# Turning a self attention head's masked weights one slot later while cross attention runs (transformer stack, one core)

## The reference, cut to what matters

```
# 1. cross attention, 16 heads of 16, x against 4096 context rows
energy = einsum('nqhd,nkhd->nhqk', q, k)
attn   = softmax(energy / E**0.5)
x = x + (einsum('nhqk,nkhd->nqhd', attn, v)) @ Wo.T + bo
# 2. self attention, 16 heads, only the 64 largest scores of a row count
scores = einsum('bhqd,bhkd->bhqk', q, k) / 4
top_scores, top_idx = top_k(scores, 64)
x = x + (softmax(top_scores) @ v[top_idx]) @ Wo.T + bo
```

## Time and profile before

| | |
|---|---|
| median of 3 runs | 1667.11 us (1654.56, 1667.11, 1667.49) |
| span of the profiled execution | 1653.0 us |
| busy PE / DVE / ACT | 1379.1 / 1325.5 / 976.1 us (83%, 80%, 59%) |
| mean granted clock of PE | 0.900 of full speed |
| head 0 of self attention starts | 215.1 us |
| first head after cross attention (p = 45) starts | 841.6 us |
| head 63 ends | 1127.9 us |

### The profile page before, as it was taken

How to read it: one execution, slowest core, us unless ns; L and a number is a source line. 1 busy time by engine, 2 the same in 40 slices (tenths; PEclk the granted TensorE clock), 3 DMA queues, 4 the chain that set the end, 5 groups by cost and what they waited for, 6 DMA issues and landing times. The chain is left out here.

```text
span 1653.0 us, 31583 instructions
## 1 busy us (share of the span) xinstructions
PE 1379.1 (83%) x11762; PEld 853.6 (52%) x11762; DVE 1325.5 (80%) x3968; ACT 976.1 (59%) x1579; POOL 273.9 (17%) x253
## 2 busy tenths in 40 slices
PE   8999899998999998999968797698669789464646
PEld 4555556665665665666644583475246336222213
DVE  1221178999799998989998999999988988888993
ACT  6678676776677776778743533456485366334420
POOL 4100012222132222222222121211100100100000
PEclk9999998999999999999979898799779899676567
DMA  7645341444022211220104122125436326223220
GB/s 150 157 116 129 66 92 38 99 96 92 14 40 53 52 21 34 53 36 18 40 24 160 52 87 67 39 80 171 131 100 172 114 60 172 72 57 109 85 56 7
DMA packets 96855, 132.67 MB, mean 80 GB/s; under 512 B 20192, under 2 KB 80872, under 8 KB 93744
## 3 DMA queue, kind: packets, MB, share of 16 engines
q1 hardware_dynamic: 96688, 130.50, 31.7%
HBM read 124.95 MB, written 5.51 MB: 79 GB/s over the span
## 5 line engine op out<-in xcount | busy, mean ns | idle before, releaser
L1325 ACT ACTIVATE attn_arena<-ps 128x1024 f32<-128x1024 f32 x512 | 496.5, 1022 | 205.9 <-PE ps L411 204.7
L1906 DVE MATCH_REPLACE8 attn_late<-attn_top,attn_late 128x256 f32<-128x256 f32 x1024 | 410.9, 409 | 0.0
L1903 DVE MAX8 attn_top<-attn_late 128x8 f32<-128x256 f32 x1024 | 380.8, 413 | 24.3 <-ACT attn_late L1347 24.3
L411 PE MATMUL ps<-attn_arena 32*128 32x256 f32 x4096 | 375.1, 408 | 8.7 <-ACT attn_arena L1325 4.3
L411 PEld LDWEIGHTS ps<-attn_arena 32*128 32x128 f32 x4096 | 253.7, 188 | 77.3 <-issue 42.7
L425 PE MATMUL ps<-attn_arena 128*32 128x256 f32 x4096 | 280.8, 391 | 1.3 <-issue 0.7
L1213 POOL TENSOR_SCALAR attn_late<-attn_late 128x512 f32<-128x512 f32 x64 | 95.6, 1494 | 602.4 <-DVE attn_late L1906 602.4
L425 PEld LDWEIGHTS ps<-attn_arena 128*32 128x32 f32 x4096 | 108.5, 110 | 135.2 <-issue 76.5
L1472 ACT ACTIVATE attn_arena<-attn_late,attn_arena 128x255 f32<-128x255 f32 x256 | 108.0, 496 | 89.4 <-DVE attn_late L1746 56.8
L686 PE MATMUL ps<-attn_arena 128*128 128x256 f32 x512 | 130.0, 400 | 17.5 <-ACT attn_arena L1427 17.4
L664 PE MATMUL ps<-attn_arena,attn_q 128*128 128x512 f32 x256 | 135.8, 660 | 5.7 <-ACT attn_arena L1413 5.5
(11 more groups left out here) (235 smaller groups left out, 1643.7 us busy)
## 6 DMA issues: line engine op xcount, KB each, us to landing
attn_arena<-ctxT SPq DMA_DIRECT2D x124, 256.0 KB, 4.7
attn_arena<-maskT SPq DMA_DIRECT2D x32, 512.0 KB, 4.4
attn_arena<-ctx SPq DMA_DIRECT2D x32, 512.0 KB, 4.1
attn_late<-rows SPq DMA_DIRECT2D x256, 64.0 KB, 2.3
attn_arena<-ctxV SPq DMA_DIRECT2D x15, 1024.0 KB, 13.0
attn_late<-wide SPq DMA_DIRECT2D x64, 128.0 KB, 2.9
attn_early<-wide SPq DMA_DIRECT2D x64, 128.0 KB, 3.5
wide<-attn_early SPq DMA_DIRECT2D x16, 256.0 KB, 3.0
```

Source lines behind the costliest of these rows:

```text
L411: mm = pe.matmul(ps[:, first + j - 2 * i, u * S:(u + 1) * S], kx[n % 2][rows, k0:k0 + P], qpad[rows, n % GROUPS, b * S:(b + 1) * S], start ...
L1325: act.activation(probs[m % 2][:, 2 * i:2 * i + 2], ps[:, first:first + 2, :], ACT.Exp, scale=1.0 / 16.0).then_inc(exp_done, 1)
L1903: dve.max(top[:, t, turn], s[:, i, t] if turn == 0 else work[:, i, t]).then_inc(picked, 1)
L1906: dve.match_replace(work[:, i, t], top[:, t, turn], s[:, i, t] if turn == 0 else work[:, i, t], LOW).then_inc(picked, 1)
```

## The change

While cross attention still runs (`crossing(p)`, true for p up to 44) the four steps of head `done` move. PE: `turn_pm` from slot 0 to the end of slot 1, behind `scores(p + 1)`; `products` from slot 2 to slot 3, behind that slot's `turn_acc`, `make_qk`, `make_v` or `project` and ahead of what `DUE` places there. ACT: `take_pT` from slot 1 to slot 2, behind `take_scores(p + 1)`; `take_sums` from the end of slot 3 to the start of slot 0 of the next period. DVE: `divide_self` from turn 1 to turn 3. The instructions, their number and their tiles are the same. From p = 45 on everything stands where it stood.

```diff
+def crossing(p):
+    return cross_it(p, 0) is not None
@@ PE
                     if slot == 0:
-                        if 0 <= done < B * H:
+                        if 0 <= done < B * H and not crossing(p):
                             turn_pm(done)
...
                             turn_x(h)
+                        if 0 <= done < B * H and crossing(p):
+                            turn_pm(done)
                     if slot == 2:
-                        if 0 <= done < B * H:
+                        if 0 <= done < B * H and not crossing(p):
                             products(done)
...
                                 make_qk(b, (q + 2) // 4)
+                        if 0 <= done < B * H and crossing(p):
+                            products(done)
@@ ACT
                     m = cross_it(p, slot)
+                    if slot == 0 and p >= 2 and crossing(p - 1):
+                        take_sums(p - 2)
...
                     if slot == 1:
-                        if 0 <= done < B * H:
+                        if 0 <= done < B * H and not crossing(p):
                             take_pT(done)
...
                             take_scores(p + 1)
+                        if 0 <= done < B * H and crossing(p):
+                            take_pT(done)
                         if ending and d == 2:
-                            take_sums(done) if done >= 0 else None
                             take_qk(h, 0)
                     if slot == 3:
                         if ending and d == 0:
-                            take_sums(done) if done >= 0 else None
                             take_misc(general[:, h:h + 1], M_[:, 0:1], "bad", h)
                         elif ending and d == 2:
                             take_scores(p + 1)
-                        elif 0 <= done < B * H:
+                        if 0 <= done < B * H and not crossing(p):
                             take_sums(done)
@@ DVE
-                    if 0 <= p - 2 < B * H and (p - 2) % HG == HG - 1:
+                    if 0 <= p - 2 < B * H and (p - 2) % HG == HG - 1 and not crossing(p - 1):
                         divide_self(p - 2)
...
                 if turn == 3:
+                    if p >= 2 and (p - 2) % HG == HG - 1 and crossing(p - 1):
+                        divide_self(p - 2)
```

## The result

The changed kernel took 1680.94 us (median of 4 runs, 1679.91 to 1682.30), the kernel before 1660.84 us (4 runs, 1648.70 to 1667.49): a ratio of 1.0157, 95% interval 1.0113 to 1.0200. It is slower, as forecast. The ratios and their intervals here rest on fast runs alone (those within 1.5% of the same kernel's fastest), while a median takes all runs, so a ratio isn't the quotient of the two medians beside it.

What follows compares the result with a forecast made beforehand. DVE's search was taken to bound heads 0 to 13, PE with its exponentials heads 17 to 44, DVE from 45. Terms +3 - 3 + 26 + 0 gave +26, span 1679, some 1681 us; 1688 was forecast, range 1664 to 1708.

Steps and rivals of the forecast that it cites:

- Slots of the plain head: PE's four slots in a plain crossing head: 2.41, 4.62, 2.41, 3.98 us, 13.42 against 12.29, +1.13 us a head.
- The value 1.64 for L571 and L579 together: Slot 1's scores plus transposes on PE: 1.64 us taken, 0.59 if they overlapped the next L411 as before.
- Heads 17 to 44: Stretch where PE is the nearer bound: 28 x 13.42 plus other blocks gives 412.8 us against 387.2, +25.6.
- Heads 0 to 13: Stretch paced by DVE, which hides the start of PE's growth: between 0 and +6.7 us, +3 taken.
- Heads 14 to 16: Stretch helped by fewer waits for masked weights and `project`: between -6 and +3 us, -3 taken.
- Waits moved: ACT's and DVE's moved steps in the crossing are covered; if one cover failed, 0 to +0.3 us a head.
- After head 44: Rest of the kernel, where DVE sets the pace: nothing moves, 0 us.
- From the span to the median: Whole kernel: span 1679 means some 1681 us for this execution; 1688 taken, between that and 1693.
- DVE's waits for copied scores: In the crossing, DVE would wait for copied scores in nearly every head, together over 50 us.
- A: Rival, crossing: PE's waits and half speed go, nothing else is paid; 17 us faster, 1650; chance 0.07.
- B: Rival, crossing: spells and waits go (29 us), offsetting re-packed slots (32 us); some +8, 1675; chance 0.25.
- C: Rival, crossing: half speed stays, nothing of 15.3 us comes back; +41, 1708; chance 0.12.

Runs made afterwards that it cites:

- e3: Changed kernel with `turn_pm` ahead of `scores(p + 1)` in slot 1 instead of behind it; 1653.05 us, ratio 1.0003 to the kernel before.
- e1: Kernel before with only `turn_pm` moved, to behind slot 1's scores; 1643.72 us, ratio 0.9919 to the kernel before.
- e2: Changed kernel with `turn_pm` back in slot 0 and `take_pT` back in slot 1; 1651.28 us, ratio 0.9997 to the kernel before.
- e8: Changed kernel, unchanged, run again; 1679.19 us, ratio 1.0182 to the kernel before.
- e4: Kernel before with only `turn_pm` moved, to slot 1 ahead of `scores(p + 1)`; 1645.92 us, ratio 0.9945 to the kernel before.

## Why the prediction was right, and where it wasn't

The forecast (slower, 1688 us, 1664 to 1708) came out at 1680.94. Its mechanism is shown: the two pieces came to stand in slots that wait themselves, the transposes parted the scores from their neighbour, and the two empty slots gave their time to nobody. That the sum of the parts came so near is luck in part: +26 was forecast for the span and +27.8 measured, but the terms are off by +4.3 (heads 0 to 13), +1.8 (14 to 16), -5.5 (17 to 44), +3.9 (after) and -2.3 us (ahead of head 0), and cancel.

- *Slots of the plain head.* Forecast 2.41, 4.62, 2.41, 3.98; measured 2.32, 4.62, 2.32, 3.97. The value 1.64 for L571 and L579 together was taken right from its two bounds (0.59 and 1.64). e3 shows what the other would have meant.
- *Heads 17 to 44.* Forecast 412.8 us, measured 407.3 and 407.0. The mis-sized term is the empty slot: 2.41 us came from a slot behind which L411 waited 0.25 us for the exponential; behind the empty slots of the changed kernel it waits 0.16, and they take 2.32. Twice 0.09 or 0.10 us in 28 heads is 5.3 us, the whole difference. The other terms held as a sum only, 407.3 - 28 x 13.23 = 36.9 us against the 37 counted: a block of eight matmuls costs 1.72 to 1.82 us (14.95 - 13.23 with `make_qk`), not 1.93, and the small ones more than 10.
- *Heads 0 to 13.* Forecast +3, measured +7.3 and +3.4. One account fits both; it is an estimate. e1 and e2, without a spell there, took 181.6 us, close to DVE's own busy time there (181.3), so the spell of 10.2 us and the gap of 1.42 us ahead of it cost the kernel before some 5.8 of its 187.4. The changed kernel without spell and without its own gap (1.4 us, last section) is at 189.4. The moved pieces so cost some 7.8 us, above my upper bound of 6.7, and the lost spell took 5.8 off that in both comparisons (7.8 - 5.8 + 1.4 = 3.4 in e8). The +3 came near the +3.4 of e8 for that reason, not for mine.
- *Heads 14 to 16.* Forecast -3, measured -1.2 and -3.4; the first execution holds a spell of 10.2 us behind the branch, e8 one of 3.4.
- *Waits moved.* All covers held: L579 waits for nothing, and e2 and e3 show `take_sums`, `take_pT` and `divide_self` without a price that can be told.
- *After head 44.* Forecast 0, measured +3.9 and +6.4. Over the ten profiled executions here, which are alike in that part, it took 810.8 to 819.3 us, so the profile of one run can't tell a difference of this size; that the change has a part in it is neither shown nor excluded.
- *From the span to the median.* This step failed. The sum gave 1681 us for this execution; the profiled one took 1682.3, and the median is 1680.9. I added 7 us because the median shown was 12.5 above the fastest run. Over 31 runs the kernel before has 1656.31, so the profiled 1654.6 stood close to its middle, and three runs had been too few. The 42 runs of the kernel before in the two sets cover 33 us, the eight of the changed one 7.5 and ten each of e2 and e3 11 and 8; why the one scatters more wasn't tried.
- *DVE's waits for copied scores.* I wrote over 50 us, in nearly every head; they are 43.0 us in 19 heads. In e8 they are 39.2 in 19. In the others DVE came to the scores late itself, behind its other work (`divide_self`, norms, logits) and its waits for that; this is my reading, and the count by plain heads didn't see it.
- *Rivals.* A fell on the ratio, though half of it was true: the waits for the masked weights did go (14.1 us), and e1, where all but one of them go too, is faster. B's 1675 us is as near to 1680.94 as my 1688; it fell on the ratio (at least 1.0113) and on heads 17 to 44 in 407 us, where it wanted under 390. C fell on the clock: with 20.5 or 6.8 us of half speed the time is the same within 2 us.

## What to carry to other kernels

In a loop whose slots are tied by a ring of two buffers, a slot is either short or waits for the one before it. Ask then of each piece not how long it is but whether the *next* slot would have waited for that long; put pieces into the slots that don't wait, leave no slot empty beside a full one, and test two harmless moves together, since their effects don't add. Where matmuls of few rows run beside the next group of their own shape, as L571 beside L415 here, keep other shapes from between them, and look which rows the two share.

## What was not expected of the hardware

In heads 0 to 13 of the changed kernel, with PE busy for 189.74 of 194.70 us, the granted clock fell to half (1.2 GHz) for 10.3 us. It fell behind a gap of 0.81 us in slot 1 of head 10 for which no engine is named; PE's timeline there:

```profile
351.64 0.86 PE L415 MATMUL ps<-attn_arena 32*128 32x256 f32 x4
353.31 1.69 PE L415 MATMUL ps<-attn_arena 32*128 32x256 f32 x6 [0.81 <-issue]
```

The same program in e8:

```profile
354.30 1.61 PE L415 MATMUL ps<-attn_arena 32*128 32x256 f32 x10 [0.16 <-ACT attn_arena L1333]
356.71 1.02 PE L415 MATMUL ps<-attn_arena 32*128 32x256 f32 x6 [0.80 <-issue]
```

The gap is there again, ahead of the same record, and the clock did not fall. e3 has it too (1.74 us) and a spell of 13.7 us behind it. Other kernels have such a gap elsewhere: the kernel before in head 2, ahead of its spell of 10.2 us at 250.0, and e4 in head 2 (2.90 us, with a spell of 3.4 us from 246.9). In the kernel before:

```profile
248.85 0.48 PE L567 MATMUL ps<-attn_late 32*128 32x256 f32 x1 [1.42 <-issue]
```

Rival C read from PE's 97% busy in the whole stretch that little idle time was enough; right ahead of that spell PE had stood idle twice, 0.97 us for the masked weights and then these 1.42. So a gap of 0.8 us was followed by a spell in one execution and not in another of the same program, and the kernel before has one of 1.9 us in head 30 with none behind it. What makes the gap stays open; it wasn't tried. The spell made the stretch 3.9 us longer, not the 5.1 that half of 10.3 would be; PE's waits for the exponentials may have taken up the rest.
